# Attention values on one Trainium2 core: the moving and the stationary operand change places, with copies and loads put in another order

## The reference

```python
q = (x @ wq.T + bq).reshape(B, S, 32, 16)   # k, v the same
scores = einsum('bshd,bstd->bsht', q, k) / sqrt(16)
context = einsum('bsht,bstd->bshd', softmax(scores), v).reshape(B, S, 512)
x = layernorm(x + context)
# w1, w2 (1376 x 512), w3 (512 x 1376): blocks of 64 weights rounded to 16 levels
# by the block's largest magnitude
h = silu(x @ dq1.T) * (x @ dq2.T)
x = layernorm(x + h @ dq3.T)
```

## Time and profile before

| | us |
|---|---|
| median of three runs | 787.29 (787.03 to 789.25) |
| the profiled execution | 788.01 |
| its span, first to last instruction | 786.2 |
| TensorE busy in the span | 732.7 |
| VectorE busy | 633.4 |
| ScalarE busy | 484.6 |

### The profile page before, as it was taken

How to read it: one execution, slowest core, us unless ns; L and a number is a source line. 1 busy time by engine, 2 the same in 40 slices (tenths; PEclk the granted TensorE clock), 3 DMA queues, 4 the chain that set the end, 5 groups by cost and what they waited for, 6 DMA issues and landing times.

```text
span 786.2 us, 14305 instructions
## 1 busy us (share of the span) xinstructions
PE 732.7 (93%) x5688; PEld 625.5 (80%) x5688; DVE 633.4 (81%) x876; ACT 484.6 (62%) x650; POOL 106.8 (14%) x101
## 2 busy tenths in 40 slices
PE   4899999966999989999999999999999999999983
PEld 4778788856999989999888877887887788888761
DVE  2699999975888988988888899999977986554386
ACT  3588979773645636546853878877756775333134
POOL 2011012113101101111101121121201111000022
PEclk9999999995555655555799999999999999999995
DMA  9964455999797695995413371211514010330347
GB/s 219 223 182 146 134 166 167 250 305 271 166 261 189 184 283 134 269 216 202 163 26 122 120 230 54 81 39 31 173 59 155 1 61 21 134 119 13 121 147 160
DMA packets 89474, 117.89 MB, mean 150 GB/s; under 512 B 24768, under 2 KB 70848, under 8 KB 86496
## 3 DMA queue, kind: packets, MB, share of 16 engines
q1 hardware_dynamic: 88272, 114.88, 51.6%
q10 hardware_dynamic: 1136, 2.10, 1.2%
HBM read 76.42 MB, written 38.86 MB: 147 GB/s over the span
## 4 chain that ended last, share of the span: by engine, by line
PE 54%; DVE 18%; issue 11%; ACT 8%; DMA 4%; SPq 4%; POOL 1%; DVEq 0%; POOLq 0%; ACTq 0%
PE ps_p L1043 10%; DVE nf_acc L1166 8%; PE ps_s L947 7%; PE ps_s L945 7%; PE ps_s L946 7%; PE ps_p L945 5%; PE ps_p L947 5%; PE ps_p L946 5%; ACT nf_y L777 4%; PE ps_s L1030 3%; PE ps_t L968 2%; DMA qk_parts<-qk_p 2%; DVE part L1298 2%; DMA k_st<-qk_parts 1%; ACT part L852 1%
## 5 line engine op out<-in xcount | busy, mean ns | idle before, releaser
L1166 DVE SCALAR_TENSOR_TENSOR nf_acc<-nf_y,nf_acc 128x1024 f32<-128x1024 f32 (+4 forms) x266 | 298.5, 1122 | 37.6 <-ACT nf_y L777 28.3
L777 ACT ACTIVATE nf_y<-nf_w,bound_b 128x1024 f32<-128x1024 f32 (+4 forms) x285 | 288.9, 1047 | 9.7 <-DVE nf_acc L1162 3.4
L1043 PE MATMUL ps_p<-probT,v_bd 128*68 128x32 f32 x1024 | 125.7, 301 | 7.9 <-issue 7.9
L1043 PEld LDWEIGHTS ps_p<-probT,v_bd 128*68 128x68 f32 x1024 | 122.7, 211 | 9.4 <-issue 8.0
L945 PE MATMUL ps_p<-x_hl,w_hl 128*128 128x512 f32 x192 | 77.6, 404 | 6.1 <-DVE w_hl L1184 4.1
L695 POOL TENSOR_TENSOR nf_w<-nf_w,nf_rec 128x1024 f32<-128x1024 f32 (+4 forms) x19 | 39.5, 2080 | 320.1 <-DVE nf_rec L1150 320.1
L1325 DVE TENSOR_TENSOR silu<-silu,ps_s 128x512 f32<-128x512 f32 (+1 forms) x44 | 30.1, 684 | 61.5 <-PE ps_s L947 61.5
L927 ACT ACTIVATE hid_hl<-silu 128x512 fp32r<-128x512 f32 (+1 forms) x44 | 27.8, 632 | 77.6 <-DVE silu L1325 77.6
L947 PE MATMUL ps_p<-x_hl,w_hl 128*128 128x512 f32 x192 | 75.5, 393 | 0.0
L945 PE MATMUL ps_s<-x_hl,f_ha 128*128 128x512 f32 x192 | 75.4, 393 | 0.0
L946 PE MATMUL ps_p<-x_hl,w_hl 128*128 128x512 f32 x192 | 75.3, 392 | 0.0
(11 more groups left out here) (110 smaller groups left out, 1253.1 us busy)
## 6 DMA issues: line engine op xcount, KB each, us to landing
x_hl<-x_parts SPq DMA_DIRECT2D x10, 2048.0 KB, 8.5
qk_parts<-qk_p SPq DMA_DIRECT2D x64, 204.0 KB, 2.6
q_st<-qk_parts SPq DMA_DIRECT2D x48, 272.0 KB, 6.8
k_st<-qk_parts SPq DMA_DIRECT2D x48, 272.0 KB, 7.2
x_parts<-x_st SPq DMA_DIRECT2D x16, 512.0 KB, 4.4
nf_w<-in_L_ffn_w SPq DMA_DIRECT2D x24, 256.0 KB, 3.0
dequantised<-nf_acc SPq DMA_DIRECT2D x10, 512.0 KB, 2.6
v_blocks<-v_t SPq DMA_DIRECT2D x16, 256.0 KB, 3.5
```

The source lines that it names most:

```text
L777: act.activation(nf_y[0:p, at % NY, 0:w], nf_w[0:p, u % 2, 0:w], ACT.Identity, bias=bound_b[0:p, i:i + 1], scale=STEEP).then_inc(s_ny, 1)
L1043: t = pe.matmul(ps_p[0:MV, (G + 3) % NPV, i * H:(i + 1) * H], v_bd[hb % 2][:, :, g * GI + i], probT[:, G % 2, i], start=True, stop=True)
L1166: dve.scalar_tensor_tensor(out=acc, in0=y, scalar=float(NF4[i + 1]), in1=acc, op0=ALU.min, op1=ALU.max).then_inc(s_nacc, 1)
```

## The change

- **Values.** `values(G)` now takes `probT[:, G % 2, i]` (128 x 32) as weights and streams the 68 columns of `v_bd`. Its output is 32 heads by 68, so four of them (i = 4a + j, j from 0 to 3) stand in the four groups of 32 partitions, and the 16 fill 4 x 68 columns of one bank. ScalarE copies these 128 x 272 to `ctmp` (`evacuate`), TensorE transposes them back in four pieces (`back`), and `context` copies from there as before. `ps_p` banks 0 and 1 take the values, 2 and 3 the transposes.
- **Padded rows.** `v_bd` has rows of 68 f32 (`VS`) in place of 64, so the 68 streamed columns stand 272 bytes apart.
- **Order.** Context comes one slot later, and so do `ct`, moments, norm and `xt`; so do the three slots with one level in `LV_A`; `BACK_AT` places `back`. On ScalarE both levels of a slot stand in front of the context copies and the exponential, where one stood before and one behind.
- **First loads.** `load_v(0)` moves into the projection loop (tau 47); the queries of the second half block are read behind it, not in the loop at tau 43 to 45.
- `pairs(g)` only writes the cutting of w3 turns in another way; they come out the same.

```diff
@@ -53,6 +53,8 @@
+    VS = TI + 4
@@ -132,15 +143,15 @@
-    FIRST_STACKS = {FIRST_LOAD + at: which for at, which in ((0, (0, 0)), (2, (0, 1)), (4, (0, 2)),
-                                                             (6, (1, 0)), (7, (1, 1)), (8, (1, 2)))}
+    FIRST_STACKS = {FIRST_LOAD: 0, FIRST_LOAD + 2: 1, FIRST_LOAD + 4: 2}
     VALUES_FREE = 3 * KC * NBK - KC
+    FIRST_VALUES = 3 * KC * NBK - 1
     LV_P = [1, 1, 1, 1, 1, 1, 1, 1, 2, 2, 2, 2] * NBK
...
     for b in range(NBK - 1):
-        LV_A[8 * b + 10:8 * b + 13] = [1, 1, 1]
+        LV_A[8 * b + 11:8 * b + 14] = [1, 1, 1]
     LV_T = (2, 3)
@@ -161,20 +172,22 @@
     HEADS = [range(0, 7), range(7, 14), range(14, 21), range(21, 28), range(28, 32)]
-    CT_AT, XT_AT, MOMENTS_AT, NORM_AT, F_AT = {}, {}, {}, {}, {}
+    CT_AT, XT_AT, MOMENTS_AT, NORM_AT = {}, {}, {}, {}
     for b in range(NBK - 1):
         for k in range(len(HEADS)):
-            CT_AT.setdefault(8 * b + 10 + k // 2, []).append(("ct", b, k))
-        MOMENTS_AT[8 * b + 12] = b
-        NORM_AT[8 * b + 13] = b
+            CT_AT.setdefault(8 * b + 11 + k // 2, []).append(("ct", b, k))
+        MOMENTS_AT[8 * b + 13] = b
+        NORM_AT[8 * b + 14] = b
         for c in range(KC):
-            XT_AT.setdefault(8 * b + 14 + c // 2, []).append(("xt", b, c))
-    LATE = {8 * b + 8 + k: 8 * b + 13 for b in range(NBK - 1) for k in range(2)}
-    CONTEXT_AT = {}
+            XT_AT.setdefault(8 * b + 15 + c // 2, []).append(("xt", b, c))
+    BACK_AT, CONTEXT_AT = {}, {}
+    LATE = {8 * b + 8 + k: 8 * b + 14 + k // 2 for b in range(NBK - 1) for k in range(4)}
     for G in range(GG):
-        CONTEXT_AT.setdefault(max(G + 3, LATE.get(G, 0)), []).append(G)
-    for G in range(GG):
+        CONTEXT_AT.setdefault(max(G + 4, LATE.get(G, 0)), []).append(G)
+        BACK_AT.setdefault(G + 4 if G % 8 == 2 and G > 8 else G + 3, []).append(G)
+    for G in range(GG + 1):
         TURNS += CT_AT.get(G, []) + XT_AT.get(G, [])
@@ -276,15 +289,16 @@
         q_st1 = sb("q_st1", [P, H, TS], BF16, att)
-        v_bd_0 = sb("v_bd_0", [P, MV, TI], F32, att)
+        v_bd_0 = sb("v_bd_0", [P, MV, VS], F32, att)
         st_1 = [q_st1, sb("k_st1", [P, H, TS], BF16, att)]
...
         ctx = sb("ctx", [MV, H, P], F32, att)
-        v_bd_1 = sb("v_bd_1", [P, MV, TI], F32, att)
+        v_bd_1 = sb("v_bd_1", [P, MV, VS], F32, att)
         x1_st = sb("x1_st", [P, 2, 2, BK], F32R, att)
+        ctmp = sb("ctmp", [P, NCT, 4 * MV], F32, att)
         v_bd = (v_bd_0, v_bd_1)
@@ -541,9 +558,14 @@
                 for q in range(Q4):
-                    sp.dma_start(v_bd[hb % 2][32 * q:32 * q + 32, DV * q:DV * q + D],
+                    sp.dma_start(v_bd[hb % 2][32 * q:32 * q + 32, DV * q:DV * q + D, 0:TI],
                                  v_d[hb].rearrange("(d t) s -> t d s", d=D)[:, :, TI * q:TI * q + TI]
                                  ).then_inc(s_ldv[hb % 2], 16)
+            def store_x1(key):
+                _, b, c = key
+                low_done(sp, key)
+                sp.dma_start(x1_d[b, :, :, c], x1_st[:, c % 2].bitcast(F32)).then_inc(s_stx[c % 2], 16)
@@ -604,11 +626,12 @@
                 if tau in FIRST_STACKS:
-                    hb, b = FIRST_STACKS[tau]
-                    load_stacks(sp, hb, [b], range(2) if hb == 0 else [0])
-            values_stored(sp, KC)
-            sp.wait_ge(s_vzero[0], 2 * Q4)
-            load_v(0)
+                    load_stacks(sp, 0, [FIRST_STACKS[tau]])
+                if tau == FIRST_VALUES:
+                    values_stored(sp, KC)
+                    sp.wait_ge(s_vzero[0], 2 * Q4)
+                    load_v(0)
+            load_stacks(sp, 1, sides=[0])
             sp.wait_ge(s_proj, 3 * KC * NBK)
@@ -834,15 +855,22 @@
+            def evacuate(G):
+                if G == 0:
+                    values_stored(act, KC * NBK)
+                act.wait_ge(s_pv, G + 1)
+                wait(act, s_back, G - NCT + 1)
+                act.activation(ctmp[:, G % NCT], ps_p[:, G % 2, 0:4 * MV], ACT.Copy).then_inc(s_evac, 1)
             def context(G):
...
                 b, e = divmod(hb, 2)
-                act.wait_ge(s_pv, G + 1)
+                act.wait_ge(s_back, G + 1)
                 if e == 0 and g == 0 and b:
...
                 act.activation(ctx[:, :, at:at + GI],
-                               ps_p[0:MV, (G + 3) % NPV].rearrange("p (i h) -> p h i", h=H), ACT.Copy
+                               ps_p[0:MV, 2 + G % 2].rearrange("p (i h) -> p h i", h=H), ACT.Copy
                                ).then_inc(s_ctx, 1)
@@ -887,10 +915,12 @@
             for G in range(GG):
+                steep(LV_A[G])
                 for at in CONTEXT_AT.get(G, []):
                     context(at)
-                steep(LV_A[G] // 2)
                 exp(G)
+                if G >= 2:
+                    evacuate(G - 2)
                 if G == 4:
@@ -900,17 +930,17 @@
                     norm_1(NORM_AT[G])
-                steep(LV_A[G] - LV_A[G] // 2)
+            context(GG - 4)
+            evacuate(GG - 2)
+            for key in XT_AT.get(GG, []) + TAIL_1:
+                high(key)
             context(GG - 3)
-            for key in TAIL_1:
-                high(key)
-            context(GG - 2)
             steep(LV_T[0])
...
                 high(key)
-            context(GG - 1)
+            evacuate(GG - 1)
+            context(GG - 2)
             steep(LV_T[1])
             for s in range(NS):
@@ -920,6 +950,8 @@
                 act.activation(silu[0:rows, s % 2], ps_s[0:rows, 0], ACT.Silu).then_inc(s_silu, 1)
+                if s == 0:
+                    context(GG - 1)
                 steep(LV_F[s][0])
@@ -1038,11 +1070,22 @@
                 pe.wait_ge(s_probT, G + 1)
-                wait(pe, s_ctx, G - NPV + 1)
+                wait(pe, s_evac, G - 1)
                 for i in range(GI):
-                    t = pe.matmul(ps_p[0:MV, (G + 3) % NPV, i * H:(i + 1) * H], v_bd[hb % 2][:, :, g * GI + i],
-                                  probT[:, G % 2, i], start=True, stop=True)
+                    a, j = divmod(i, 4)
+                    t = pe.matmul(ps_p[32 * j:32 * j + 32, G % 2, a * MV:(a + 1) * MV], probT[:, G % 2, i],
+                                  v_bd[hb % 2][:, :, g * GI + i], start=True, stop=True)
                 t.then_inc(s_pv, 1)
+            def back(G):
+                pe.wait_ge(s_evac, G + 1)
+                wait(pe, s_ctx, G - 1)
+                for a in range(4):
+                    t = pe.transpose(ps_p[0:MV, 2 + G % 2, P * a:P * a + P], ctmp[:, G % NCT, a * MV:(a + 1) * MV],
+                                     ident[:])
+                t.then_inc(s_back, 1)
@@ -1102,22 +1145,28 @@
                 scores(G)
+                if G >= 2:
+                    values(G - 2)
                 for key in CT_AT.get(G, []):
                     turn(key)
-                if G >= 2:
-                    values(G - 2)
+                for at in BACK_AT.get(G, []):
+                    back(at)
                 for key in XT_AT.get(G, []):
...
             values(GG - 2)
-            for key in TAIL_1:
+            for key in XT_AT.get(GG, []) + TAIL_1:
                 turn(key)
+            back(GG - 3)
             values(GG - 1)
...
                 turn(key)
+            back(GG - 2)
...
                 gate_up(s)
+                if s == 0:
+                    back(GG - 1)
                 for key in F_TURNS.get(s, []):
```

36 lines of the change are left out of this document (22 added, 14 removed).

## The result

| | before | after |
|---|---|---|
| median, us | 787.62 | 791.90 (787.84 to 795.75) |
| ratio to before | 1 | 1.0056 (1.0038 to 1.0073) |
| the profiled execution; its span | 788.01; 786.2 | 794.03; 792.2 |
| span to scores of slot 4 | 193.5 | 194.9 |
| slots 4 to 31 | 165.3 | 163.4 |

What follows compares the result with a forecast made beforehand. TensorE was taken to bound attention slots (6.19 us of work, 6.12 measured), VectorE right behind. 788.0 - 15.4 (slots) - 2.7 (start) = 769.9, stated as 769 since the runs' median is 0.7 lower; range 761 to 797.

Steps and rivals of the forecast that it cites:

- Values: TensorE, attention slots: two records of a matmul run one behind the other, 16 steps of 129 ns, 2.07 us for 3.94.
- the bounds of 1.0 and 4.1 us: Values of a slot on TensorE: 1.0 us if all four groups run side by side, 4.1 if nothing overlaps.
- The case in which the stride comes on top: Values' strided stream: 252 ns a step, 4.0 us a slot; held by the no-overlap rival's chance, 0.14.
- Back and the copy: Added per attention slot: four f32 transposes on TensorE, 0.97 us, and one ScalarE copy of 272 columns, 0.4 us.
- the clock's rival: Attention: TensorE's clock rises, TensorE takes at most 4.4 us a slot, VectorE bounds at 5.21 plus 0.1; 763 us, chance 0.15.
- I take 5.55: Slots 4 to 31: TensorE at 5.29, VectorE at 5.21, plus a quarter us for lumps; 15.4 us saved from 6.12.
- the case that I had named at the end: Attention: if values take 2.1 us but slots stay above 5.9, the two-engine bound is the step that fell.
- The context copies: ScalarE's longest queue, two context copies and four normalising activations: TensorE's `back` waits for the first copy, costed at nothing.
- The tail: From 358.8 to 380 us: 2.7 us off TensorE, x1 turns one slot later; taken as 0 (minus 3 to plus 3).
- The start: Before slot 4: earlier v_bd loads move its scores from 193.46 to about 190.8 us, saving 2.7 (0 to 7.4).
- The levels in front: Both ScalarE levels before the exponential: VectorE's lifts find theirs ready, ending 18.4 us of nf_y waits; exponential delay hides.
- the chain or the DMA taking over: Attention: DMA work of 5.0 us a slot or the values-copy-`back`-copy chain bounds; slot 5.85, 778 us, chance 0.12.

Runs made afterwards that it cites:

- e3: The changed kernel with all 16 value matmuls of a slot written to one group, partitions 0 to 31; 800.1 us, ratio 1.0156.
- e4: The changed kernel with rows of `v_bd` left at 64 f32, so streamed columns stand 256 bytes apart; 821.7 us, ratio 1.0414.
- g1: The changed kernel with 32 score matmuls of 64 columns a slot in place of 64 of 32 (layer not computed); 783.9 us, ratio 0.9959.
- e5: The changed kernel with SyncE issuing a slot's x1 stores ahead of its stack loads; 791.0 us, ratio 1.0040.
- e1: The changed kernel with query and key loads of half blocks 2 to 7 cut to one 512-byte row each (layer not computed); 779.9 us, ratio 0.9894.
- f4: The changed kernel with contexts ahead of levels, VectorE's lift ahead of x1 low parts, x1 stores ahead of stack loads, old first-load order; 786.2 us, ratio 0.9972.
- e7: The changed kernel with the first loads in their old order; 790.1 us, ratio 1.0021.
- e8: The changed kernel with one level of a slot in front of the exponential and one behind, as before; 799.6 us, ratio 1.0156.
- e9: The kernel before with one edit: both ScalarE levels of a slot in front of context copies and exponential; 783.3 us, ratio 0.9960.

## Why the prediction was wrong

**Values, right way, too timid.** The two halves of a matmul do not serialise: 1.2 us a slot, near the bound of 1.0, not 2.07. That the bounds of 1.0 and 4.1 us held is luck, since I had scaled them by a clock that the values don't follow (1.2 us at 0.50 and at 1.00). The case in which the stride comes on top, 252 ns a step, is out: 129 ns in one group (e3). What the Trainium skill says under "SBUF — State Buffer", section "Door 1: The DMA port swizzle", of accesses that cross to a new 16-byte line does not tell 256 from 272 bytes; the runs do (e4).

**Back and the copy, right.** 0.84 against 0.97, 0.38 against 0.4. The clock rose too, to 0.76, as the clock's rival said, but with TensorE off the bound that gave no time back: its 763 needed slots at VectorE's 5.21 plus 0.1.

**VectorE's slot, right; "I take 5.55" was the step that fell.** It is the case that I had named at the end: values under 2.1 us and slots above 5.9. VectorE's work is 5.15 us a slot, forecast 5.21. I gave a quarter of a us for the lumps and got 0.9: 6.05. The mistake was to compare the means of two engines when three other things could end a slot: the transfers, TensorE's instruction blocks and ScalarE's row of activations. The first I had seen and given 0.12; the DMA engines are 0.89 busy after. In slots 4 to 31 they cost less through late data than through TensorE's own instructions, a rival that I did not have (about 8 us by g1; e5, which takes most of the waits for x1 stores away, gained 1 at most, and e1, without the loads, gives 12 for all their effects). I had used TensorE's 160 busy us of 165 as evidence that loads are in time; but the kernel before took 3.94 us for 32 values records, and had that long to fetch the next block. That this is why it never stopped for one is argued, not shown.

**The context copies, "so I cost it at nothing".** This is the second step. ScalarE's row of eight activations holds `back`, `back` holds x1, x1 holds VectorE: 13.3 us of waits. f4, with that wait at 1.7 us, has slots 4 to 31 shorter by 9.4 us. The tail, for which I had taken 0, is 24.5 to 30.4 us in all new kernels and 19.7 to 21.2 in all old ones; what of it is ScalarE's row and what the delay of everything by a slot was not separated.

**The start.** -2.7 forecast, +1.4 measured, and e7 shows the new order to be the cause: what slot 4 needs, the second keys, was put behind the six loads of `q_st1`, 1.6 MB, that used to be done by then.

**The levels in front** did what I had said in the new kernel; e8 prices it at 7.7 us. But I had called VectorE's wait for nf_y free while TensorE is the bound, and e9 gains 0.4% in the kernel before.

The sum: 769.9 + 13.5 (slots) + 5.3 (tail) + 4.1 (start) + 1.2 (feed-forward) = 794, the profiled execution. The feed-forward stage takes 405.8 or 407.5 us in the profiled executions of the variants. The difference is TensorE's clock at its start, 0.66 in the first 5 us of the kernel after and 1.00 in those of e1 (405.8 us), so its 1.2 says little. The rival nearest the truth was the chain or the DMA taking over, and I had priced it at a slot of 5.85, where 6.05 came.

## What to carry to other kernels

When the bound of a stage is removed, the next slot time need not be the larger of the remaining means. List every engine, the DMA engines and the instruction queues near the new bound, and follow the one slot in which the most is queued on the lightest engine: here ScalarE, with 3.45 us of work a slot in the mean, held up the other two. Before making a busy engine faster, ask whether its instructions will come as fast; when a trace says "issue" in the middle of a run of matmuls, count the records between the stops and look at the packets of the instruction queue. And try the cheap half of a change by itself: here the order of ScalarE gained, and the rest of the change lost.

## What the runs showed of the hardware

- f32 matmuls with 32 output partitions overlap in four groups: 40 ns for a record of 68 streamed columns, 129 ns in one group at a clock of 0.97 (e3). A phase of 32 records in four groups takes 1.2 us at a granted clock of 0.50 and of 1.00.
- Streaming f32 at 256 bytes between columns costs 65 ns a record where 272 bytes cost 40 (e4), and the other engines are slower beside it: `shift` 1316 ns in place of 652, lifts and ScalarE's levels by 14 and 22%. The weight load at the same stride did not do that (`shift` 652 ns in the kernel before).
- TensorE stopped 1.4 to 4.6 us at 11 block borders of 254 instructions with the DMA engines 0.89 busy, and went on 1.3 to 1.6 us after the packet of its instruction queue had landed. With the stack loads gone (0.39 busy, e1) two such stops are left between 193 and 380 us, with fewer instructions (g1) none.
